# An attention and mixture-of-experts decoder on one core: the first expert tile of the last step is loaded in another order, and the joins' fetches are issued at most four ahead

## The reference

```python
logits = xf @ gate_w + gate_b
probs = jax.nn.softmax(logits, axis=-1)
gates, expert_idx = jax.lax.top_k(probs, K)          # K = 2 of E = 8
h = jax.nn.relu(jnp.einsum('nc,ech->neh', xf, w1) + b1)
expert_out = jnp.einsum('neh,ehc->nec', h, w2) + b2
out = sum over the token's two experts of gate * expert_out
x = _layernorm(x + out, axis=-1)
```

## Time and profile before

| | |
|---|---|
| runs | 979.92, 980.39, 985.46 us; median 980.39 |
| profiled execution, its own time | 977.83 us |
| profiled execution, span from the first to the last instruction | 976.0 us |
| mean granted TensorE clock | 0.967 |
| PE, DVE, ACT, POOL busy | 864.4, 627.1, 493.7, 292.4 us |
| last expert weights issued / last matmul ends / last ACT instruction ends | 926.7 / 946.4 / 970.8 us |

### The profile page before, as it was taken

How to read it: one execution, slowest core, us unless ns; L and a number is a source line. 1 busy time by engine, 2 the same in 40 slices (tenths; PEclk the granted TensorE clock), 3 DMA queues, 4 the chain that set the end, 5 groups by cost and what they waited for, 6 DMA issues and landing times.

```text
span 976.0 us, 19714 instructions
## 1 busy us (share of the span) xinstructions
PE 864.4 (89%) x7316; PEld 685.4 (70%) x7316; DVE 627.1 (64%) x1876; ACT 493.7 (51%) x1147; POOL 292.4 (30%) x470
## 2 busy tenths in 40 slices
PE   3568898999999979989989999999999999969970
PEld 2346677668777766677767777877777878859970
DVE  4998776775867478875767776587884554410036
ACT  1335445455555664354565544655645456435542
POOL 4422323211342215340212331241331122412244
PEclk9779999999999999999999999999999999989995
DMA  9996000000010000000000021320210134789973
GB/s 325 393 340 211 2 1 12 12 7 1 28 34 24 18 11 24 17 29 6 12 7 22 12 83 50 110 99 28 93 66 29 55 93 143 252 314 404 361 289 103
DMA packets 35086, 100.49 MB, mean 103 GB/s; under 512 B 4888, under 2 KB 19488, under 8 KB 34432
## 3 DMA queue, kind: packets, MB, share of 16 engines
q1 hardware_dynamic: 31584, 89.91, 26.7%
q0 software_dynamic: 3408, 9.34, 2.5%
HBM read 86.48 MB, written 32.30 MB: 122 GB/s over the span
## 4 chain that ended last, share of the span: by engine, by line
PE 62%; DVE 20%; ACT 7%; issue 6%; POOL 2%; DMA 1%; SPq 0%; another core or an unknown queue 0%; POOLq 0%; ACTq 0%; DVEq 0%
PE ps L735 43%; PE ps L740 7%; PE ps L747 5%; PE ps L811 3%; DVE PT L1134 2%; DVE stat L1075 2%; ACT PT L1498 2%; ACT slot_rows L1498 1%; PE ps L878 1%; PE ps L1036 1%; DVE sm L1091 1%; DVE PT L1099 1%; DVE stat L1076 1%; ACT L1580 1%; ACT PT L1580 1%
## 5 line engine op out<-in xcount | busy, mean ns | idle before, releaser
L1687 POOL TENSOR_TENSOR stat<-stat,mhalf 128x1 f32<-128x1 f32 x112 | 67.0, 598 | 292.5 <-DVE stat L1077 292.1
L735 PE MATMUL ps<-wall,slot_rows 128*128 128x256 f32 (+1 forms) x448 | 130.7, 419 | 11.8 <-ACT KB L1525 9.1
L735 PEld LDWEIGHTS ps<-wall,slot_rows 128*128 128x128 f32 x448 | 78.6, 192 | 35.8 <-issue 22.4
L740 PE MATMUL ps<-cst,PT 128*128 128x128 f32 x512 | 73.4, 280 | 17.9 <-DVE PT L1134 4.2
L1134 DVE TENSOR_REDUCE PT<-ps 128x8 f32<-128x1024 f32 x64 | 75.4, 1220 | 12.5 <-PE ps L747 12.4
L747 PE MATMUL ps<-KB 32*128 32x128 f32 (+1 forms) x2048 | 76.9, 287 | 7.1 <-DVE PT L1134 2.4
L747 PEld LDWEIGHTS ps<-KB 32*128 32x128 f32 (+1 forms) x2048 | 64.9, 190 | 25.7 <-issue 20.5
L740 PEld LDWEIGHTS ps<-cst,PT 128*128 128x128 f32 x512 | 58.6, 143 | 33.3 <-issue 16.2
L735 PEld LDWEIGHTS ps<-slot_rows,wall 128*128 128x128 f32 x640 | 75.3, 192 | 9.1 <-issue 3.9
L735 PE MATMUL ps<-slot_rows,wall 128*128 128x128 f32 x640 | 79.0, 277 | 2.5 <-ACT PT L1580 0.9
L735 PE MATMUL ps<-wgu,slot_rows 128*128 128x352 f32 x256 | 79.5, 462 | 0.8 <-ACT slot_rows L1460 0.6
(11 more groups left out here) (248 smaller groups left out, 1805.9 us busy)
## 6 DMA issues: line engine op xcount, KB each, us to landing
EW<-moe_w SPq DMA_DIRECT2D x25, 514.0 KB
EW<-moe_w SPq DMA_DIRECT2D x25, 512.0 KB
PT<-moe_w SPq DMA_DIRECT2D x11, 514.0 KB
PT<-moe_w SPq DMA_DIRECT2D x11, 512.0 KB
wall<-wts SPq DMA_DIRECT2D x1, 4104.0 KB, 20.1
slot_rows<-ys_d SPq DMA_DIRECT2D x10, 384.0 KB, 9.6
work<-xs_d SPq DMA_DIRECT2D x27, 129.0 KB
Y<-xTg SPq DMA_DIRECT2D x16, 128.0 KB, 2.7
```

Source lines behind the costliest of these rows:

```text
L735: last = k.e.matmul(o, a, b, start=(i == 0), stop=(i == len(pairs) - 1))
L740: last = k.e.transpose(ps[:, u.at, c * P:(c + 1) * P], src[:, c * P:(c + 1) * P], ident)
L1687: return k.e.tensor_tensor(v[:, 7:8], v[:, 8:9], mhalf[:, :], ALU.pow)
```

## The change

Four edits. `early_turns` gives another order: weights up and down of tile 19, rows of 19, rows of 20, then for each following tile its weights and the rows of the tile behind it. In `plan_tiles` the weights of tiles of the last step no longer need that all samples are sent, only the table. In `plan_join` a fetch from sample 4 on needs the fetch four before it, and its estimated duration is 3.5 us rather than 6.0. In `sp_join` SP waits for that earlier fetch.

```diff
 def early_turns():
-    yield from ((what, x) for x in range(NT) for what in ("rows", "load up", "load down") if early(what, x))
+    one = SURE[-2]
+    order = [("load up", one), ("load down", one), ("rows", one), ("rows", one + 1)]
+    for x in range(one + 1, NT):
+        order += ("load up", x), ("load down", x), ("rows", x + 1)
+    yield from ((what, x) for what, x in order if x < NT and early(what, x))
@@ plan_tiles
-                        needs=[("table", b), *[(n, "sent") for n in range(STEPS[b])], *last * (y is not None),
+                        needs=[("table", b), *[(n, "sent") for n in range(STEPS[b] if what == "rows" or not last_step(x) else 0)], *last * (y is not None),
@@ plan_join
-            yield piece(work=[("S", 0.5, None), ("Q", 1.1, None), ("L", 6.0, (n, "fetched"))], alone=True,
-                        needs=[(n, "b2" if n in KEPT else "saved"), ("table", len(STEPS) - 1), *(("stored", x) for x in range(tiles_of(n)))])
+            yield piece(work=[("S", 0.5, None), ("Q", 1.1, None), ("L", 3.5, (n, "fetched"))], alone=True,
+                        needs=[(n, "b2" if n in KEPT else "saved"), ("table", len(STEPS) - 1), *(("stored", x) for x in range(tiles_of(n))),
+                               *[(n - 4, "fetched")] * (n >= 4)])
@@ sp_join
                     many = 2 if n in KEPT else 3
+                    if n >= 4:
+                        k.wait_ge(fetched[n - 4], 16)
```

## The result

The changed kernel takes 974.9 us (median of 6, 972.90 to 976.37), the kernel before 980.8 us (median of 6, 979.81 to 985.46) beside it. The ratio is 0.994, with a 95% interval of 0.9918 to 0.9962: 5.9 us less, within the 1% that had the chance of 0.90. The forecast was 975.3, so its total holds. Its two terms don't hold equally well, and the later runs make the gain itself smaller than 5.9; the last sections are about that.

A forecast was written before the change was run, and what follows sets the result against it. Rows 22's landing was taken to set the last step's end on PE, then POOL and DVE the joins. Gains 2.5 + 2.6 = 5.1 us off 977.83 give 972.7; with the 2.6 us profile-to-median difference, 975.3, range 972 to 979.5.

The forecast's parts named there:

- The joins' order: Joins at the kernel's end: add 1 moves from behind store 36 to behind store 35, gain 2.6 us.
- The walk on POOL: Step-by-step timing of POOL's adds, roots and stores in the joins: store 38 ends at 950.05, before at 950.04.
- The throttle, worth nothing: Fetches for the joins: holding each until the one four before has landed gains nothing by itself.
- The start, 2.5 us at turn 22: Head of the last step: earlier weights 19 bring turn 22 from 877.4 to 874.9; bounds 1.6 and 5.1 us.
- the backlog of bytes: Head of the last step: fewer bytes ahead of rows 22; if it counts for nothing, the gain is 1.6 us.
- need at least the 2.3 us from their issue: Head of the last step: rows 19 and 20 land at 862.6 and 863.7, up 19 starts 5.1 us earlier.
- 3.47 MB, 8.7 us at 0.4: Bytes the DMA engines must move before turn 22, against 4.75 MB and 11.9 us before: 3.2 us less.
- The clock rival: PE's clock falls in the 2.9 us before turn 22, costing 1.0 to 3.4 us: 976.3 to 978.7; chance 0.2.
- The scatter held back: Last step's head: early weights delay the last scatter and SP's row, losing 2.0 of 2.5 us: 977.3; chance 0.1.
- PE keeps the 5.1: Last step: PE keeps all 5.1 us gained at up 19 if DMA engines catch up: 972.7; chance 0.1.
- Only one of the two gains shows: Either the joins' or the start's gain fails to show: 977.8 or 977.9; chance 0.1.
- Slower through four at a time: Fetches become the bound past 6.6 us to landing each; at 9.6 us the kernel takes 987.5; chance 0.05.

The follow-up runs named there:

- joins_only: Kernel before with only the planner's 3.5 us for fetches and SP's wait for the fetch four before, the start as before: 976.22 us, ratio 0.9978.
- throttle_only: Kernel before with only SP's wait for the fetch four before, every order unchanged: 979.39 us, ratio 1.0.
- no_throttle: Changed kernel without SP's wait for the fetch four before, the planner's order kept: 974.31 us, ratio 0.9964.
- after: The changed kernel itself, with all four edits, against the kernel before: 974.9 us, ratio 0.994.
- after_again: The changed kernel once more, unaltered, in the second batch, against the kernel before: 974.56 us, ratio 0.9948.
- start_only: Only the start changed (weights of tile 19 ahead of the scatter wait), fetches and joins as in the kernel before: 976.42 us, ratio 0.9991.
- up19_twice: Changed kernel with up 19's product computed twice, keeping PE busy longer at no new bytes: 974.46 us, ratio 0.9967.
- one_at_a_time: Changed kernel with SP holding each fetch until the one directly before has landed: 989.83 us, ratio 1.0094.
- up20_early: Changed kernel with up 20's weights also ahead of the scatter wait, rows 19 to 21 together, down weights later: 973.31 us, ratio 0.9932.
- rows24_ahead: up20_early with the last stretch's first loads, 2 MB of weights among them, moved behind turn 20 and its following rows: 972.44 us, ratio 0.9927.

## Why the prediction was right, and which terms were off

**The joins' order, 2.6 us.** It measured 2.85 (24.42 to 21.57), and within 0.03 of 21.57 in every profile with the new order and the fetches free to run, against 24.4 to 24.7 with the old; in the times of joins_only it is 2.2 (0.7 to 3.6). The walk on POOL was right: store 38 is at 950.03 - 943.61 = 6.42 us behind the last matmul's start, where it was at 949.00 - 942.75 = 6.25 before, and sample 6's add on DVE comes at 7.09 rather than 9.95, 2.86 earlier. The walk on DVE gave 2.8 at sample 6's add and 2.5 at join 7, and I took 2.6, between them; the first was the better one. ACT's scaling ahead of the ReLU cost nothing, as said.

**The throttle, worth nothing.** throttle_only has 1.0 (0.9983 to 1.0017), and no_throttle keeps 21.56.

**The start, 2.5 us at turn 22.** This is the term that was mis-sized. The three profiles with the old start have turn 22 at 20.45, 20.23 and 21.97, mean 20.9; the six with weights 19 first and rows 19 and 20 behind them (after, after_again, start_only, no_throttle, up19_twice, one_at_a_time) are at 18.50 to 20.93, mean 19.6. That is 1.3 us, below my lower bound of 1.6. At the last matmul it is 89.8 against 89.15, so 0.7 is left when the clock's share is off; with three and six profiles that spread over 1.7 and 3.6 us this is not clear of nothing, and start_only's times say 0.9 (-0.5 to 2.2). The same profiles show where the term went. SP issued rows 22 at 11.6 to 12.6 us behind the table, mean 12.0, where it was 13.4 to 13.7 with the old start, mean 13.6: 1.6 us earlier, as the sum had it. From there they took 6.8 to 8.4 us to land, mean 7.5, against 6.5 to 8.2, mean 7.2. So, as far as these nine profiles tell, the shift of SP's issues is all that was gained, and the 0.9 us that the backlog of bytes was to add aren't there. Two steps of the working failed:
- "need at least the 2.3 us from their issue". It was a lower bound, and I used it as the value. Rows 19 and 20 took 4.5 us with weights 19 in flight, so up 19 came 3.6 us earlier and not 5.1.
- "3.47 MB, 8.7 us at 0.4". The engines moved 282 to 294 GB/s until 870 and 403 only from there. The bytes of 859.3 to 870 are 3.08 MB; at 403 GB/s they need 7.6 us, and they took 10.7. I counted bytes at full rate and not the pause of 4 us in which SP issues no weights while it waits for the scatter. But the pause is at most half of the loss: a share of 0.87 to 0.88 rather than 1.02 makes some 1.5 of the 3.1 us, by my estimate from these windows, and from 860 to 866 the share was 0.89 to 0.97, with one dip to 0.65 (199 GB/s) at 866 to 867. The rest is fewer bytes for the same share, as in the window at 1.02 and 300 GB/s before; why is open.

**The clock rival, 0.2.** It came true in part, and more often than I gave it: behind turn 22, where I had it, a stretch at the lower level cost 1.5 to 1.6 us in three profiles of seven, within the 1.0 to 3.4 of the rival, and 0.3 to 0.5 in two more. (The window 948 to 949 at 0.79, on which I argued, is not among rows 3; the profile of before has it.) In the first profile it struck one tile earlier, behind turn 21. There up 20's extra 1.3 us were hidden but for 0.5, since the rows of 22 weren't there anyway; nor did the clock stay at 1.0 from 862 to 880, as I had expected.

**The scatter held back, 0.1.** Not seen: the last scatter took 4.4 to 5.2 us in the seven profiles where only weights 19 stand ahead of its wait, and 4.7 to 5.1 in the four without. In up20_early, with up 20's weights ahead as well, it took 5.4; one profile doesn't tell whether that is chance. The Trainium skill has each DMA engine take turns between the queues that have work for it ("DMA: Bandwidth & Descriptors", section "Queues, rings and completion order"), and by that rule the scatter would be slower; no run here shows a cost of it.

**PE keeps the 5.1.** Its condition was that the DMA engines catch up. They don't; turn 22 waits for its rows in every profile with this order. rows24_ahead shows what it takes: the rows ahead of the weights, at both places. It gives 3.5 us at the last matmul against the old start (86.28 in one profile, 89.8).

**Only one of the two gains shows, 0.1.** This is nearer to what happened than its chance says: the joins gave theirs, and the start by itself is not clear of nothing in its times. I had the two as equals.

**Slower through four at a time.** The price L is 4.2 us (4.2 to 5.5 over all profiles with four in flight), against the 6.6 from which it would cost.

**The sum.** By the profiles it is 2.85 + 0.7 = 3.5 us, and no_throttle (3.5 us less), up19_twice (3.2) and the two parts added (0.9 + 2.2 = 3.1) agree with that. The whole change has 5.9 (3.7 to 8.0) and 5.1 (3.1 to 6.9) by the ratios of its two comparisons. But the changed kernel's own time hardly moves: 974.90 and 974.56, with 974.31 in no_throttle. What moves is the kernel before: 980.80 over the six runs beside the first comparison, 977.79 to 978.88 over the 80 later ones. By the medians after_again is 3.4 us faster, which is the sum of the parts. So the 5.9 is most likely some 2 us too much, from six runs of before that came out high; that the two parts do something together isn't excluded, as the intervals overlap.

That the forecast of 975.3 came so near is therefore in part luck. The gain of 5.1 was some 1.6 us too large, through the start, where 0.7 stands for 2.5. The base from which it was taken, 980.39, the median of three runs, was 1.5 to 2.6 us above what the later batches gave. The two errors cancel.

## What to carry to other kernels

When transfers are moved forward, write down SP's issues as a series and follow the one transfer that the engine waits for: here its issue moved by 1.6 us, and that was all that PE got, whatever went out ahead of it. Put the small rows that the next tile waits for ahead of the megabyte of weights that it needs later, and follow the wait to the place where it turns up next. And compare two profiles from a mark just ahead of the change, not from the start of the program; here 2.3 us of difference lay in code that was the same. Take the base of a forecast from many runs: three runs of this kernel stood 1.5 to 2.6 us above the medians of the later ones. When a planner orders the engines, compare the orders of all of them too before a ratio is put down to the edit.

## What the runs showed of the hardware

- The DMA engines, with weights, rows and an indirect scatter in flight, moved 294 GB/s at a share of 0.88 (859.3 to 864.3 in after) and 282 at 0.87 (864.3 to 870), and 403 at 1.02 from 870 to 877.7. The share makes up for about half of the difference; a window of before had 300 GB/s at 1.02.
- A fetch of 384 KB takes 3.0 us to landing alone, 4.2 to 5.5 with up to four in flight and 6.9 to 9.6 with ten (medians of the pages). Joins that use them in order end at the same time with four or with ten (21.57 and 21.56 us behind the last matmul).
- Profiles with the same work have the stretch at the lower clock at different places: 872.3 to 875.7 in after (13.0 us behind the table), 864.3 to 867.7 and 874.5 to 878.0 in after_again (8.8 and 19.0), 865.4 to 868.8 and 879.0 to 882.5 in no_throttle (8.1 and 21.7). In before it is one stretch, 866.7 to 873.5 (9.7).
